# A two-layer perceiver block with ternary feed-forward and top-2 experts on one core: first-stage loads reordered, ternary rounding moved within pairs, experts' first units split earlier, token loads issued by POOL

## The reference

```python
x = x + softmax((n @ Wq) (ctx @ Wk).T / 16) @ (ctx @ Wk @ Wv)      # L0 cross attention
x = x + causal_softmax((n @ Wq) (n @ Wk).T / 8) @ (n @ Wv)         # L0 self attention, 64-wide queries
x = x + bit_linear(silu(conv3(bit_linear(n, w1))), w2)             # L0 ffn: 256 -> 1024 -> 256
x = x + cross attention with 16 heads over ctx @ W_kv, then W_proj # L1
x = x + causal self attention with 16 heads, then W_O              # L1
x = x + sum over 8 experts of mask * expert(n) * mean gate         # L1 ffn, each token in its top 2
```

## Time and profile before

| | us |
|---|---|
| median of 3 runs | 2734.28 (2726.33 to 2735.12) |
| the profiled execution | 2731.11 |
| its span, first to last instruction | 2729.4 |
| PE busy | 2522.3 (92%) |
| DVE busy | 1702.9 (62%) |
| ACT busy | 1377.1 (50%) |
| POOL busy | 836.4 (31%) |
| mean granted clock of PE | 0.969 |

### The profile page before, as it was taken

One profiled execution on the slowest core, in us unless ns is written; L12 is line 12 of the kernel. 1 busy time (PEld: TensorE's weight loads), 2 busy tenths in 40 slices (PEclk: granted clock), 3 DMA queues, 4 the chain that ended last, 5 costly groups with the idle time before them and its releaser, 6 DMA issues.

```text
span 2729.4 us, 75620 instructions
## 1 busy us (share of the span) xinstructions
PE 2522.3 (92%) x32404; PEld 2169.6 (79%) x32404; DVE 1702.9 (62%) x3035; ACT 1377.1 (50%) x2201; POOL 836.4 (31%) x857
## 2 busy tenths in 40 slices
PE   6999886789999999999999999999999976999997
PEld 3566556678888888888888888888888855999997
DVE  3467778436566565575665655756756555777775
ACT  1233434445565555555555555555556523555563
POOL 1010003333344434433434344344343300111111
PEclk9999997899999999999999999999999976999999
DMA  9876740460011001100100011001001102666664
GB/s 345 314 307 266 284 178 25 145 212 26 26 42 38 30 30 38 42 30 26 49 31 30 30 38 42 30 26 54 26 30 40 55 2 99 211 200 206 207 202 145
DMA packets 61265, 283.47 MB, mean 104 GB/s; under 512 B 5137, under 2 KB 36242, under 8 KB 46354
## 3 DMA queue, kind: packets, MB, share of 16 engines
q1 hardware_dynamic: 52818, 268.73, 27.5%
q0 software_dynamic: 8160, 10.29, 2.5%
HBM read 247.45 MB, written 33.65 MB: 103 GB/s over the span
## 4 chain that ended last, share of the span: by engine, by line
PE 55%; DVE 13%; issue 13%; DMA 7%; POOL 7%; ACT 4%; SPq 0%; POOLq 0%; DVEq 0%; ACTq 0%
PE PS L1439 7%; PE PS L1275 5%; PE PS L1263 5%; DVE mpart L1809 3%; PE PS L1184 3%; PE PS L1252 3%; PE PS L1250 3%; PE PS L1251 3%; POOL ctx_lo L603 3%; PE PS L1435 3%; DMA unit_raw<-in_experts 3%; DMA sum_d<-scaled,xg 2%; POOL k_lo L595 2%; PE PS L1241 2%; DMA ctx_raw<-in_ctxT 2%
## 5 line engine op out<-in xcount | busy, mean ns | idle before, releaser
L1809 DVE TENSOR_REDUCE mpart<-PS 128x1 f32<-128x802 f32 (+1 forms) x512 | 484.7, 986 | 213.8 <-PE PS L1263 212.8
L921 ACT ACTIVATE probs<-PS 128x1024 f32<-128x1024 f32 (+1 forms) x416 | 413.4, 1025 | 217.8 <-PE PS L1439 217.8
L603 POOL TENSOR_TENSOR ctx_lo<-ctx_raw,ctx_hi 128x801 fp32r<-128x801 f32 x128 | 225.9, 1775 | 375.0 <-ACT ctx_hi L856 366.4
L595 POOL TENSOR_TENSOR k_lo<-probs,k_hi 128x400 fp32r<-128x400 f32 (+1 forms) x256 | 250.8, 980 | 275.2 <-ACT k_hi L844 275.2
L1439 PE MATMUL PS<-qbd_hi,k_hi 64*128 64x256 f32 (+1 forms) x1664 | 313.6, 374 | 0.0
L1263 PE MATMUL PS<-k_hi,qbd_hi 128*128 128x512 f32 (+2 forms) x1024 | 265.5, 361 | 22.7 <-DVE mpart L1809 12.7
L843 ACT COPY probs<-PS 128x400 f32<-128x400 f32 (+1 forms) x256 | 126.4, 494 | 244.7 <-PE PS L1243 215.3
L1275 PE MATMUL PS<-probs,vals 128*32 128x64 f32 x13312 | 233.8, 221 | 4.2 <-issue 4.0
L1250 PE MATMUL PS<-wkv_hi,ctx_hi 128*128 128x256 f32 (+1 forms) x832 | 236.5, 284 | 0.0
L1439 PE MATMUL PS<-qbd_lo,k_hi 64*128 64x256 f32 (+1 forms) x1664 | 234.5, 278 | 2.0 <-issue 2.0
L1439 PE MATMUL PS<-qbd_hi,k_lo 64*128 64x256 f32 (+1 forms) x1664 | 234.3, 278 | 0.0
(11 more groups left out here) (319 smaller groups left out, 6250.8 us busy)
## 6 DMA issues: line engine op xcount, KB each, us to landing
unit_raw<-in_experts SPq DMA_DIRECT2D x46, 1536.0 KB, 7.0
ctxN<-in_ctxN SPq DMA_DIRECT2D x16, 3328.0 KB, 11.0
ctxT<-in_ctxT SPq DMA_DIRECT2D x16, 3204.0 KB, 11.3
ctx_raw<-in_ctxT SPq DMA_DIRECT2D x64, 801.0 KB, 4.5
slots_d<-pad_rows SPq DMA_DIRECT2D x18, 1040.0 KB, 12.4
xg<-slots_d SPq DMA_DIRECT2D x23, 260.0 KB, 2.8
x<-in_x SPq DMA_DIRECT2D x1, 2048.0 KB, 10.1
sum_d<-x SPq DMA_DIRECT2D x1, 2048.0 KB, 13.8
```

The source lines that it names most:

```text
L595: g.tensor_tensor(k_lo[:, n, a, c:c + width], k_raw[p % 2][:, 0:width], k_hi[:, n, a, c:c + width].bitcast(F32), ALU.subtract).then_inc(s. ...
L603: g.tensor_tensor(ctx_lo[:, a, cols], ctx_raw[:, cols], ctx_hi[:, a, cols].bitcast(F32), ALU.subtract).then_inc(s.ctx_lo_ready, 1)
L921: act.activation(probs[rows, t % PROBS, :], PS[rows, 1024 * (t % 2):1024 * (t % 2) + 1024], ACT.Exp).then_inc(s.pr_ready, 1)
L1809: v.tensor_reduce(mpart[:, pair, half:half + 1], PS[:, at:at + width], AX, ALU.max).then_inc(s.mx_red, 1)
```

## The change

It has three parts.

1. First stage. Raw weights and w1, w2 get buffers of their own (in the three feed-forward buffers). SP loads in another order: the three weights (`first_in`), two tiles of x (`x_first`), the first ctxT and ctxN, the first layer's small weights, four tiles of x (`x_more`), w1, contexts of pairs 1 and 2, w2, pair 3, the rest of x (`x_rest`), pair 4, the second layer's weights (`b_weights_in`), the small loads of w_cp, and then pairs 5 to 15 in the loop. PE makes fold, then the first queries, then vout, then pair 0; it sums over partitions for w1 after pair 1 and for w2 after pair 3. DVE takes the absolute sums in pairs 1 and 3, the scales in pairs 2 and 4, and rounds w1 in pair 4 and w2 in pair 6, in each case after the mask of the self attention and before its feed-forward step.
2. Experts' first units. ACT rounds the down part of unit 0 together with its wide part, and all of unit 1 after tile 3 of the last `finish`; DVE takes their remainders at the matching places.
3. Token loads. Tiles 3 to 22 are loaded by POOL, after `add_tile` of the tile two before; SP keeps tiles 0 to 2 and the units.

```diff
@@ sync
-            for dst, src in first_loads:
+            for dst, src in fold_loads:
                 sp.dma_start(dst, src).then_inc(s.first_in, 16)
+            sp.dma_start(x[:, 0:X_FIRST, :], io["x"][:, 0:X_FIRST, :]).then_inc(s.x_first, 16)
...
+            def load_pair(i):
+                sp.wait_ge(s.scores_ps, i)
+                sp.dma_start(ctxT[:, :, :], pair_of(io["ctxT"], i)).then_inc(s.ctxT_in, 16)
+                sp.wait_ge(s.av_ps, i)
+                sp.dma_start(nkeys, pair_of(io["ctxN"], i)).then_inc(s.ctxN_in, 16)
...
+            sp.dma_start(nkeys, pair_of(io["ctxN"], 0)).then_inc(s.ctxN_in, 16)
+            for dst, src in a_loads:
                 sp.dma_start(dst, src).then_inc(s.weights_in, 16)
+            sp.dma_start(x[:, X_FIRST:X_MORE, :], io["x"][:, X_FIRST:X_MORE, :]).then_inc(s.x_more, 16)
+            sp.dma_start(w1_raw, io["w1T"]).then_inc(s.w1_in, 16)
+            load_pair(1)
+            load_pair(2)
+            sp.dma_start(w2_raw, io["w2T"]).then_inc(s.w2_in, 16)
+            load_pair(3)
+            sp.dma_start(x[:, X_MORE:TILES, :], io["x"][:, X_MORE:TILES, :]).then_inc(s.x_rest, 16)
+            load_pair(4)
+            for dst, src in b_loads:
+                sp.dma_start(dst, src).then_inc(s.b_weights_in, 16)
...
             def load_tile(i):
-                if i >= TOKEN_BUFS:
-                    sp.wait_ge(s.xgT_ps, i - TOKEN_BUFS + 1)
-                    sp.wait_ge(s.added, 16 * SUBS * (i - TOKEN_BUFS + 1))
...
                     load_unit(2 * i + 1, first)
-                    if i + 1 >= TOKEN_BUFS and i + 1 < SLOT_TILES:
-                        load_tile(i + 1)
@@ gpsimd
+            def load_tile(i):
+                g.wait_ge(s.xgT_ps, i - TOKEN_BUFS + 1)
+                row = g.value_load(row_u[0:1, i:i + 1], min_val=0, max_val=REGIONS * REGION - SLOT_TILE)
+                g.dma_start(xg[i % TOKEN_BUFS][:, :, :], slots_d[bass.ds(row, SLOT_TILE), :].rearrange("(s p) c -> p s c", p=P))\
+                 .then_inc((s.more0_in, s.more1_in, s.more2_in)[i % TOKEN_BUFS], 16)
+
+            g.wait_ge(s.experts_ready, 2)
             for i in range(SLOT_TILES):
                 add_tile(i)
+                if i and i + 2 < SLOT_TILES:
+                    load_tile(i + 2)
@@ scalar
             act.wait_ge(s.consts_ready, NCONST)
+            act.copy(reload[:, :], eps[:, :])
...
             round_wide(0)
+            round_down(0)
             for tile in range(PLACES + KEY_TILES):
                 finish(tile)
+                if tile == 3:
+                    round_wide(1)
+                    round_down(1)
@@ tensor
+            pe.wait_ge(s.weights_in, A_WEIGHTS_IN)
+            pe_pair_a(1)
             pe.wait_ge(s.tern_sum, 1)
-            pe.matmul(bank(2, 2), ones[:, :], small[:, 86:88], start=True, stop=True).then_inc(s.tern_ps, 1)
+            pe.matmul(bank(3, 1), ones[:, :], small[:, 86:87], start=True, stop=True).then_inc(s.tern_ps, 1)
+            pe_pair_a(2)
+            pe_pair_a(3)
+            pe.wait_ge(s.tern_sum, 2)
+            pe.wait_ge(s.tern_read, 1)
+            pe.matmul(bank(3, 1), ones[:, :], small[:, 87:88], start=True, stop=True).then_inc(s.tern_ps, 1)
@@ vector, in vec_pair_a(i) after mask_s()
+                if i in (1, 3):
+                    tern_sum(i // 2)
+                if i == 2:
+                    tern_scale(0)
+                if i == 4:
+                    tern_round(0)
+                if i == 6:
+                    tern_round(1)
                 ffn(2 * i)
@@ vector, before the experts
             rest_of_wide(0)
+            rest_of_down(0)
             for window in range(0, PLACES + 12, 2):
                 finish(window, x[:, TILES - 1, :], ids[:, TILES - 1, :], True, 32 * (TILES - 1))
+                if window == 2:
+                    rest_of_wide(1)
+                    rest_of_down(1)
```

More of the change, by code:

```diff
@@ L358, in build @@
         S_ = {n: sem(n) for n in """
-            first_in weights_in consts_ready ctxT_in ctxN_in ctxB_in wkv_in out_stored
+            first_in x_first x_more x_rest w1_in w2_in tern_read weights_in b_weights_in consts_ready ctxT_in ctxN_in ctxB_in wkv_in out_stored
             vec_step pool_step ln_var ln_rstd xn_ready xn_ps xnT_ready xs_ready xs_ps xsT_ready
@@ L377, in build @@
         NCONST = 22
-        raw = ctxNf
+        raw = hidden_f[2][:, :, :].rearrange("p t n -> p (t n)")
         wqT_raw, wkT_raw, wv_raw = (raw[:, 512 * n:512 * n + 512].rearrange("p (k n) -> p k n", k=KT) for n in range(3))
[L382 to L390, removed]
+        w1_raw, w2_raw = (hidden_f[n][:, :, :].rearrange("p t n -> p (t n)") for n in range(2))
+        fold_loads = [(wqT_raw, io["w_xqT"]), (wkT_raw, io["w_xkT"]), (wv_raw, io["w_xv"])]
+        a_loads = [(w[n][:, :, :], io["w_" + n]) for n in A_WEIGHTS] + [(convw[:, :, :], io["conv_w"]), (convb[:, :], io["conv_b"])]
+        b_loads = [(w[n][:, :, :], io["w_" + n]) for n in WEIGHTS if n not in A_WEIGHTS] + [(wo[:, :, :], io["w_o"])]
+        X_FIRST, X_MORE = 2, 6
+        FIRST_IN = 16 * len(fold_loads)
+        A_WEIGHTS_IN = 16 * len(a_loads)
+        B_WEIGHTS_IN = 16 * len(b_loads)
         XDONE_A = 2 * TILES
@@ L416, in _ @@
             sp.dma_start(w_cp4[HD:HD + 1, 0, :], io["b_p"][0:1, :]).then_inc(s.cp_in, 16)
[L417 to L421, removed]
+            with sp.Fori(5, TILES) as i:
+                load_pair(i)
             def load_ctx(n, a):
@@ L829, in _ @@
             copy_qkT()
+            act.wait_ge(s.fold_ps, 2)
+            act.copy(vout[:, :, :].rearrange("p k n -> p (k n)"), bank(1)).then_inc(s.fold_ready, 1)
             for i in range(TILES):
@@ L1014, in _ @@
                     round_x((u + 1) // 2)
-                if u + 1 < UNITS:
+                if u and u + 1 < UNITS:
                     round_down(u + 1)
@@ L1046, in _ @@
             mm.then_inc(s.fold_ps, 1)
[L1047 to L1051, removed]
+            pe.wait_ge(s.fold_ready, 1)
             def transpose_xn(to=0):
@@ L1122, in ffn @@
                     pe.wait_ge(s.xf_ready, TPC * (f + 1))
+                    if f == 0:
+                        pe.wait_ge(s.tern_read, 2)
                     if f >= 2:
@@ L1199, in pe_pair_a @@
                 ffn(2 * i + 1)
+                if first:
+                    pe.wait_ge(s.fold_ready, 2)
                 pe.wait_ge(s.attT_ready, T["attT"].up())
@@ L1584, in normalize, with tern_sum, tern_scale, tern_round @@
                 return v.tensor_scalar(xn, xi, mv[:, 0:1], rstd[:, 1:2], ALU.subtract, ALU.mult)
-            v.wait_ge(s.first_in, FIRST_IN)
+            v.wait_ge(s.x_first, 16)
             v.wait_ge(s.consts_ready, NCONST)
             layer_norm(x[:, 0, :]).then_inc(s.xn_ready, 1)
[L1589 to L1600, removed]
+            tern = ((w1_raw, w1q), (w2_raw, w2q))
+            def tern_sum(n):
+                v.wait_ge((s.w1_in, s.w2_in)[n], 16)
+                v.tensor_reduce(small[:, 86 + n:87 + n], tern[n][0], AX, ALU.add, apply_absolute_value=True).then_inc(s.vec_step, 1)
+                v.wait_ge(s.vec_step, own())
+                v.tensor_copy(carrier_v[:, :], eps[:, :]).then_inc(s.tern_sum, 1)
+            def tern_scale(n):
+                mean, inv, step = (small[:, 80 + 2 * k + n:81 + 2 * k + n] for k in range(3))
+                v.wait_ge(s.tern_ps, n + 1)
+                v.tensor_scalar(mean, bank(3, 1), 1.0 / (HID * D), 1e-5, ALU.mult, ALU.max).then_inc(s.tern_read, 1)
+                v.wait_ge(s.tern_read, n + 1)
+                v.reciprocal(inv, mean).then_inc(s.vec_step, 1)
+                v.tensor_scalar(step, mean, 1 / 127, None, ALU.mult).then_inc(s.vec_step, 1)
+                v.wait_ge(s.vec_step, T["step"].up(2))
+            def tern_round(n):
+                r, q = tern[n]
                 v.tensor_scalar(r, r, small[:, 82 + n:83 + n], MAGIC, ALU.mult, ALU.add).then_inc(s.vec_step, 1)
@@ L1771, in _ @@
             vec_pair_a(0)
-            v.wait_ge(s.weights_in, WEIGHTS_IN)
-            for i in range(1, TILES):
+            v.wait_ge(s.weights_in, A_WEIGHTS_IN)
+            v.wait_ge(s.x_more, 16)
+            for i in range(1, X_MORE - 1):
+                vec_pair_a(i)
+            v.wait_ge(s.x_rest, 16)
+            for i in range(X_MORE - 1, TILES):
                 vec_pair_a(i)
```

40 lines of the change are left out of this document (22 added, 18 removed).

## The result

| | before | after |
|---|---|---|
| median, us | 2734.49 (2726.33 to 2735.12, 4 runs) | 2864.72 (2863.0 to 2865.57, 4 runs) |
| the profiled execution, us | 2731.11 | 2864.16 |
| its span, us | 2729.4 | 2862.5 |
| mean granted clock of PE | 0.969 | 0.950 |

The ratio is 1.0478, with a 95% interval of 1.0466 to 1.0491: slower, 0.7 us from the predicted 2864.0. The spans differ by 133.1 us, and the traces of before and after put more than all of it into the experts' loop (+142.0), while the rest of the kernel is 8.9 us shorter.

The account below looks back on a forecast made before the run. TensorE (PE) was taken to bound the experts' loop, with every wait put in front of it adding in full. Terms: 2731.1 + 142 (token loads) - 8 (first stage) - 0.7 (first units) = 2864 us, range 2780 to 2910.

Parts of the forecast that it names:

- PE's wait for tokens, a tile: Experts' loop: tokens loaded by POOL land 5.6 us after PE wants them, between bounds of 2.7 and 6.8.
- clock, a tile: Experts' loop: PE restarts at a lower clock after each wait, costing 1.9 us, between bounds of 0.7 and 2.5.
- floor of the pitch: Experts' loop: the time of a tile when PE never waits, 17.6 us against 17.985 before.
- token loads, total: Experts' loop: 20 token loads moved to POOL raise the pitch from 17.985 to 25.1 us, +142 us.
- start of the first stage: First stage: loads in another order bring scores 9.8 us earlier and DVE takes them 2.2 sooner, -12.0 us.
- w1 in pair 4: First stage, pair 4: DVE's rounding of w1 exceeds its idle time, mostly covered by PE's queries, +0.5 us (0 to 1.7).
- w2 in pair 6: First stage, pair 6: DVE's rounding of w2 finds no idle time before line 1764, +2.5 us (0.5 to 3.8).
- units, DVE's and ACT's part: Experts' first units: DVE's remainder of unit 0 costs +0.9 us, ACT's wait for unit 3 goes, -1.6 us.
- Rivals 2 (late briefly): Experts' loop: POOL's load behaves as SP's did, 2.7 us late, pitch 21.2, +64, time 2786 us; chance 0.16.
- 4 (faster): Experts' loop: tokens land within 5.55 us of the scaling, PE never waits, pitch 17.6, time 2715 us; chance 0.05.
- 5 (same): Experts' loop: tokens late by about half a microsecond, gains and losses cancel, 2723 to 2739 us; chance 0.02.
- rival 3: Experts' loop: slow descriptors or queueing behind the adds, tokens 9 us late, pitch 28.5, +210, time 2933 us; chance 0.07.

Follow-up runs that it names:

- the filled wait: The changed kernel with 22 matmuls of constants put on PE ahead of its wait for the tokens of tiles 3 and later: 2830.99 us, ratio 1.0364.

## Why the prediction was right

The mechanism held, and so did the term that decides. That the time came within 0.7 us is luck in part: several steps were off and cancelled, and the runs of before alone spread over 9 us. By its steps, in us against before:

| step | predicted | measured |
|---|---|---|
| PE's wait for tokens, a tile | 5.6 | 5.36 |
| clock, a tile | 1.9 | 2.1 (394.82 - 352.82 over 20), of which the filled wait gave back 1.65 |
| floor of the pitch | 17.6 | 17.64 (352.82 / 20, loads ahead of the adds) |
| token loads, total | +142 | +142.0 |
| start of the first stage | -12.0 | -11.9 |
| w1 in pair 4 | +0.5 | +0.8 (lead 11.7 at pair 3, 9.8 at pair 4, 10.9 at pair 5) |
| w2 in pair 6 | +2.5 | +2.4 (lead 10.9 at pair 5, 7.6 at pair 6, 8.5 at pair 7) |
| transfers between pairs | +1 | +0.6 (the rest of the way from 11.9 to 8.1; that the transfers are the cause isn't shown) |
| first stage, pair 15 | -8 | -8.1 |
| units, DVE's and ACT's part | +0.9, -1.6 | +1.35 (lead 6.8 at the first expert matmul), -1.5 (8.3 at the first add), then -0.5 at the second |

**Token loads.** Two halves of the wait were off and cancelled. The load was to start 5.5 us after the scaling, 0.7 of it for reading the row number; it starts 4.25 after, before the second add's record has ended, and the row number costs nothing that shows. It was to land 5.65 us later (5.55 + 5.6 - 5.5); it took 6.7 in the turn shown and in the median. So 4.25 + 6.7 - 5.55 = 5.4 stands for the predicted 5.6. Both sizes rest on a step that failed. The start was put too late because the row number was taken to be read after the adds; POOL reads it during the first add, as the MOVE of line 733 at 2335.0 shows in the turn whose first add starts at 2334.33 and takes 1.75. The landing was taken short of the add's 6.92 because part of the unit load would be through by then; it is nearly the whole of it, and the load lands some 1.2 us after the unit. That the unit load beside it is what makes it long was right: with that nearly taken away the landing is 4.2, nearer to the lower bound than to the upper. What the prediction overlooked is that SP's 2.8 us, its lower bound, also had a unit load beside it, but behind it; the trace of before has two loads by SP behind a unit load, those of tiles 1 and 2, and they took 6.4 and 5.9 us. These were the nearer rows.

The estimate from the Trainium skill (page "DMA: Bandwidth & Descriptors", section "Anatomy of one DMA — SWDGE (gpsimd) path") of 2.6 us for this load would have given +60. The runs show 6.7 us behind the unit load, 4.2 nearly without it, and 3.3 at the least; the measurement decides. The rule of its section "Issuing engines are not separate DMA queues" holds in this case: the same load ran no faster from POOL, and all that the move can give is what it frees on SP, 8 us, and only from the right place in POOL's order.

**The clock.** 1.9 us was a choice between the bounds 0.7 and 2.5, whose middle is 1.6, and it came within 0.2 us of what was measured. The rows nearest in length would have given as much: 3.04 - 1.64 = 1.4 us after 6.03 idle, and 2.5 in the stage's first window.

**First stage.** The sum of its start was met by two misses that cancelled. The weight products were to start near 7.5 and start at 5.04. The chain from there to the scores was to take 9.2 us and takes 12.05 (17.09 - 5.04), because it doesn't run through the weights: PE waits 1.73 us for the first normalized tokens, whose tile of x landed at 8.30, and the second product takes 3.62 us where the row of before has 2.36. The size varies too. Eight other traces of this document's kernels have the same first stage up to pair 3; their weighing of pair 0 is 10.3 to 13.9 us earlier than before's. In the seven of them that round w2 on DVE, pair 15 is 3.9 to 9.0 us earlier. That 11.9 and 8.1 lie so near to 12.0 and 8 is luck within that spread. w1's rounding is firm, 0.8 in all eight traces that have it so: pair 4 lost 1.9 of its lead and pair 5 had 1.1 back, the cover by PE's queries that the +0.5 counted on. w2's costs 3.3 to 3.4 at pair 6 in all of them, as the missing bracket at 175.48 had said. What happens in pair 7 differs: the change had 1.0 back, the seven others lost 0.1 to 1.3 more. So from pair 5 to pair 7 it is 2.4 to 4.7, and the predicted +2.5 is its low end.

**Units.** Too small to be told by a time (0.9992, 0.9982 to 1.0002). In the traces both halves have their predicted signs.

Rivals 2 (late briefly), 4 (faster) and 5 (same) are out by the 20 waits of 5.36, rival 3 by the landing. Rival 4's deciding point, tokens within 5.55 us of the scaling, is met by the version with the load ahead of the adds, and it gave what that rival worked out: 2713 and 2717 against 2715.

## What to carry to other kernels

Before a load is moved to another engine, write down the instruction behind which it will stand there, when that one is released, and when the data is wanted: here the distance was 5.55 us, the way 11.0 (4.25 to the load, 6.7 to its landing), and moving it up in the same queue, ahead of two adds and of what they wait for, turned +130 us into some -19. Then look which large load it will stand behind, on whatever engine: take the landing time of a small load from a row with the same neighbour on the same side. The view of a tile mixes the landings of all DMAs that touch it, here loads and adds (4.5 to 8.6 us), and the view of the load's own line doesn't (6.4 to 7.3). Work that must run on POOL beside a busy DVE is to be read in DVE's rows too. A wait on PE costs more than its length: look for the granted clock behind it.

## What the runs showed of the hardware

- **The order against a large load decides the landing of a small one.** The same 260 KB took 2.7 to 4.0 us issued by SP just ahead of a load of 1.5 MB, 3.3 to 4.2 issued by POOL 0.7 us ahead of it, 6.9 and 7.5 issued 0.4 us ahead. Behind it they took 6.4 and 5.9 by SP and 6.4 to 7.3 by POOL, and landed 0.3 to 1.9 us after the large one. With the large load cut to 128 KB they took 4.0 to 4.4.
- **POOL's record of a plain load is 0.77 us, and 1.37 right behind a scatter-add,** of which 0.56 overlap the add's record in the turn shown. With the load first, it is the second add that grows, to 2.8 to 3.2 us from 1.54.
- **A plain load's record on POOL begins 1.0 us later than an add's would** (2.15 against 1.16 us after the scaling), the read of the row number included; behind a first add that time doesn't show.
- **DVE stands still behind POOL.** An elementwise instruction of DVE from SBUF to SBUF of 0.41 us took 2.09, 7.20 and 5.46 when it started 0.04 to 0.06 us after passes of 1.99, 7.10 and 5.37 on POOL, three times out of three. The Trainium skill, page "SBUF — State Buffer", section "Who interferes with whom", says that an instruction of DVE in a mode with two ports and one of GpSimd take a shared pair of ports for their whole length, and that the second blocks. The three pairs of rows agree with it; that this instruction of DVE ran in such a mode no row shows.
